# Second attention of a two-layer decoder, taken by batches within two pairs of heads, with the bidirectional attention of the first batch beside its last steps

## What is computed

```python
# experts: every expert on every token, weighted by its gate
h_mid = gelu(einsum('th,ehf->etf', x, moe_w1)); expert_out = einsum('etf,efh->eth', h_mid, moe_w2)
# layer 1, self-attention ("second attention"): 16 heads of 64
scores = einsum('bhqd,bhkd->bhqk', q, k) + position_bias
out = einsum('bhqk,bhkd->bhqd', softmax(scores), v); x = x + out @ wo
# layer 1, bidirectional attention: hc are the normed tokens, hq the 77 context rows
Sim = (hc @ w1)[:, :, None] + (hq @ w2)[:, None, :] + einsum('bid,bjd->bij', hc * w3, hq) + b_sim
hq_hat = einsum('bij,bjd->bid', softmax(Sim, 2), hq)
hc_bar = einsum('bi,bid->bd', softmax(max(Sim, 2), 1), hc)
x = x + concat([hc, hq_hat, hc * hq_hat, hc * hc_bar]) @ W_qv + b_qv
```

## Time and profile before

| | |
|---|---|
| runs shown | 509.86, 511.59, 510.97 us; median 510.97 |
| the profiled execution | 511.17 us, span 509.1 us |
| up to the last experts | 0 to 187 us |
| last experts, norm, first projections | 187 to 218 us |
| steps of the second attention with scores | 218 to 439 us |
| last steps, bidirectional attention | 439 to 478 us |
| norm and feed-forward | 478 to 509 us |

### The profile page before, as it was taken

One profiled execution on the slowest core, in us unless ns is written; L12 is line 12 of the kernel. 1 busy time (PEld: TensorE's weight loads), 2 busy tenths in 40 slices (PEclk: granted clock), 3 DMA queues, 4 the chain that ended last, 5 costly groups with the idle time before them and its releaser, 6 DMA issues.

```text
span 509.1 us, 12379 instructions
## 1 busy us (share of the span) xinstructions
PE 454.2 (89%) x4396; PEld 318.5 (63%) x4396; DVE 372.3 (73%) x1005; ACT 287.0 (56%) x618; POOL 122.3 (24%) x203
## 2 busy tenths in 40 slices
PE   3779878887787998599999999999999999999897
PEld 1234556666663766347676676677676767888756
DVE  3757858998767799677767778686777777447666
ACT  3752325564346796377767667676776766313460
POOL 5050000270014467102322243132311211111200
PEclk9979879998987999699999999999999999998999
DMA  7298914500000130100100000000000000000001
GB/s 214 59 98 98 101 14 140 181 4 1 0 2 23 41 103 1 32 1 1 32 4 1 1 15 15 0 0 0 0 0 0 1 1 3 1 2 1 1 0 42
DMA packets 15616, 15.74 MB, mean 31 GB/s; under 512 B 1348, under 2 KB 12859, under 8 KB 15579
## 3 DMA queue, kind: packets, MB, share of 16 engines
q1 hardware_dynamic: 15579, 15.24, 14.5%
HBM read 10.52 MB, written 4.72 MB: 30 GB/s over the span
## 4 chain that ended last, share of the span: by engine, by line
PE 71%; DVE 20%; ACT 4%; issue 3%; DMA 1%; DVEq 0%; SPq 0%; ACTq 0%
PE bank L865 16%; PE bank L1308 11%; PE bank L1261 9%; PE bank L1197 5%; PE bank L1302 5%; PE bank L1161 3%; PE bank L1148 3%; PE bank L1211 3%; PE bank L1193 2%; DVE PX L1608 2%; DVE mx L1606 2%; PE bank L974 1%; PE bank L1420 1%; PE bank L870 1%; DVE stats L1447 1%
## 5 line engine op out<-in xcount | busy, mean ns | idle before, releaser
L779 ACT ACTIVATE SN<-SN,nmx 128x512 f32<-128x512 f32 x128 | 92.9, 726 | 9.4 <-DVE nmx L1808 8.4
L528 POOL TENSOR_TENSOR CTX<-YT 128x128 f32 (+1 forms) x64 | 29.4, 459 | 197.2 <-DVE YT L1806 197.2
L865 PE MATMUL bank<-cs,SN 128*128 128x128 f32 x512 | 67.5, 274 | 1.6
L865 PEld LDWEIGHTS bank<-cs,SN 128*128 128x128 f32 x512 | 57.0, 141 | 17.2 <-issue 11.5
L1261 PE MATMUL bank<-TK,TQ 64*128 64x512 f16 x384 | 52.6, 380 | 0.0
L1793 DVE CUSTOM_DVE_ANT_0 SN<-bank,strip 128x512 f32<-128x512 f32 x64 | 43.3, 677 | 1.3 <-PE bank L1261 1.3
L1808 DVE CUSTOM_DVE_ANT_0 SN<-bank,strip 128x512 f32<-128x512 f32 x64 | 43.6, 682 | 0.0
L1801 DVE COPY PTO<-bank 128x512 f32<-128x512 f32 x32 | 22.1, 692 | 23.8 <-PE bank L1308 23.8
L1801 DVE COPY Z<-bank 128x512 f32<-128x512 f32 x32 | 22.1, 692 | 23.4 <-PE bank L1308 23.3
L787 ACT COPY PTO<-bank 128x512 f32<-128x512 f32 x32 | 18.8, 586 | 29.5 <-PE bank L1308 29.5
L787 ACT COPY Z<-bank 128x512 f32<-128x512 f32 x32 | 18.8, 586 | 27.3 <-PE bank L1308 27.3
(11 more groups left out here) (300 smaller groups left out, 906.3 us busy)
## 6 DMA issues: line engine op xcount, KB each, us to landing
bias_rows<-biasr SPq DMA_DIRECT2D x1, 4096.0 KB, 44.4
band<-bias_rows SPq DMA_DIRECT2D x1, 3072.0 KB, 13.0
wqkv<-in_twqkv SPq DMA_DIRECT2D x8, 192.0 KB, 2.7
w1s<-in_w SPq DMA_DIRECT2D x8, 128.0 KB, 2.3
w2s<-in_w SPq DMA_DIRECT2D x8, 128.0 KB, 2.1
wB<-in_wb SPq DMA_DIRECT2D x1, 753.0 KB, 6.2
wA<-in_wa SPq DMA_DIRECT2D x1, 520.0 KB, 5.2
X<-in_x SPq DMA_DIRECT2D x2, 256.0 KB, 3.2
```

The source lines that it names most:

```text
L779: sc.activation(p, p, ACT.Exp, bias=nmx[:, r % RING, h:h + 1], scale=-1.0, accum_out=psm[:, r % RING, h:h + 1]).then_inc(sm["exp_ready"], 1)
L865: return nc.tensor.transpose(out_, in_, ident[0:n, 0:n])
```

## The change

The rows are taken in groups of four: within two pairs first batch 0 of both, then batch 1 of both (where, pair_of). Projections come per group, three in four steps; only q, k and v of the first group stand ahead of or in step 0. The norm of batch 1 ahead of the attention, the last half output of expert 7 with its sum, and the high and low part of its input move into steps 0 to 3; the last expert is taken in halves of tokens, with 14 matmuls on ones between them. CTX and wo are kept as f16 high and low parts, so that GpSimd does three operations per row instead of one and an output tile is 24 f16 matmuls instead of 8 f32 ones. RAW moves from YT to wC. Output tiles 0 to 3 stand in steps 12 to 15 and 4 to 7 in steps 18 to 21 of the last pass; the norm, similarities, softmax and context of batch 0 stand between them in steps 15 to 21, and batch 1 alone follows. The bias b_qv is added into X by GpSimd.

```diff
-FIRST_OUT = ROWS + LAG
+OUT_TILE = {12: 0, 13: 1, 14: 2, 15: 3, 18: 4, 19: 5, 20: 6, 21: 7}
+OUT_BANK = (7, 7, 7, 7, 7, 3, 7, 5)
...
-PROJECTIONS = [("q", 0), ("k", 0), ("q", 1), ("k", 1), ("v", 0), ("v", 1)]
-JOBS = len(PROJECTIONS)
-SPLIT_JOBS = 4
+JOBS = 3
+LOWS = 2
+GROUPS = BODY // TG
 JOB_BANK = 7
-FIRST_BANKS = (6, 7, 4, 5, 6, 7)
-JOBS_FROM = 1
+FIRST_BANKS = (5, 3, 6)
+YP_BANK = (4, 6)
+LAST_ORDER = (0, 2, 1, 3)
...
-            CTX = t5("CTX", [P, PAIRS, TOK])
-            RAW = YT[:, :].rearrange("p (r c) -> p r c", c=2 * P)
+            CTX = t5("CTX", [P, PAIRS, 2, TOK], F16)
...
+            WOP = t5("WOP", [P, 2, PAIRS * P], F16)
+            RAW = wC[:, :].rearrange("p (r c) -> p r c", c=2 * P)
...
+            pool.wait_ge(sm["ld_band"], 16)
             for u in range(2):
                 for part in range(2):
                     split_part(0, u, part)
+                for part in range(6):
+                    strip_part(u, u, part)
+            wo = WO[:, :, :].rearrange("p n c -> p (n c)")
+            pool.wait_ge(sm["ld_wo"], 16)
+            gp.tensor_tensor(WOP[:, 0, :], wo, ones[:, 0:1].to_broadcast([P, PAIRS * P]), ALU.mult).then_inc(sm["ow_ready"], 1)
+            pool.wait_ge(sm["ow_ready"], 2)
+            gp.tensor_tensor(WOP[:, 1, :], wo, WOP[:, 0, :], ALU.subtract).then_inc(sm["ow_ready"], 1)
...
                     pool.wait_ge(sm["raw_ready"], n - 4)
-                    gp.tensor_tensor(dst, raw[:, 0:P], raw[:, P:2 * P], ALU.mult).then_inc(sm["ctt_ready"], 1)
+                    gp.tensor_tensor(CTW[:, :], raw[:, 0:P], raw[:, P:2 * P], ALU.mult).then_inc(sm["ctw_ready"], 1)
+                    pool.wait_ge(sm["ctw_ready"], 2 * n - 9)
+                    gp.tensor_tensor(dst[:, 0, :], CTW[:, :], ones[:, 0:1].to_broadcast([P, P]), ALU.mult).then_inc(sm["ctw_ready"], 1)
+                    pool.wait_ge(sm["ctw_ready"], 2 * n - 8)
+                    gp.tensor_tensor(dst[:, 1, :], CTW[:, :], dst[:, 0, :], ALU.subtract).then_inc(sm["ctt_ready"], 1)
...
-                    part = s - (LAG + 2 * u)
...
                     if part in (0, 1) and not last:
...
+                            pool.wait_ge(sm["pj_mm"], (i * GROUPS + u + 3) * JOBS)
...
+                    part = 2 * (s - (ROWS + TG * (u + 1) + 1))
...
+                if last and s == ROWS + TG + 6:
+                    add_bias(0)
+
+            def add_bias(g):
+                t = slice(TG * g, TG * g + TG)
+                pool.wait_ge(sm["ln_y"], TAIL + 1 + 2 * g)
+                b = row("b_qv").rearrange("p (o d) -> p o d", o=1).to_broadcast([P, TG, P])
+                gp.tensor_tensor(X[:, t, :], X[:, t, :], b, ALU.add).then_inc(sm["xb_ready"], 1)
...
+                for p in (2 * half, 2 * half + 1):
+                    gelu(NE - 1, p, LAST_ORDER[p])
+                for p in (2 * half, 2 * half + 1):
+                    high(NE - 1, 1, p, LAST_ORDER[p])
...
+            rstd_of(5, 0)
+            norm_high(0)
...
+                if s == 0:
+                    high_part(3, 2, 0, 0, FIRST_BANKS[2])
...
-                if last and s == FIRST_OUT + 4:
+                if s == 1:
+                    rstd_of(5, 1)
+                if s == 3:
+                    norm_high(1)
+                if last and s == 16:
+                    rstd_tiles(TAIL + 1, 0, TG)
+                if last and s == 17:
...
+                    take_tiles(1, 0, TG)
+                if last and s == 18:
+                    similarity_exp(0)
+                if last and s == 19:
+                    take_ast(0)
+                if last and s == 20:
+                    maxima_exp(0)
+                    take_context(0)
+                if last and s == 21:
                     rstd_tiles(TAIL + 2, TG, TG - 1)
...
-            similarity_exp(0)
-            take_tiles(2, TG, TG - 1, 3)
+            t5_steps(act, t5_step)
+            take_tiles(2, TG, TG - 1)
             rstd_tiles(TAIL + 3, NT - 1, 1)
-            take_tiles(3, NT - 1, 1, 4)
-            take_ast(0)
-            maxima_exp(0)
+            take_tiles(3, NT - 1, 1)
             similarity_exp(1)
-            take_context(0)
+            take_ast(1)
+            rstd_tiles(TAIL + 4, 0, TG)
             maxima_exp(1)
-            take_ast(1)
             take_context(1)
-
...
-            hidden(NE - 1, 1)
-            for u in range(2):
-                expert_out(NE - 2 + u, u)
...
+            last_hidden(0)
+            pe.wait_ge(sm["hid_lo"], (NE - 2) * 4 + 4 + 4)
+            pe.wait_ge(sm["acc_ready"], 2 * NE - 3)
+            half_out(NE - 2, 0, 0, 5)
+            last_hidden(1)
+            pe.wait_ge(sm["hid_lo"], (NE - 1) * 4 + 2 + 4)
+            half_out(NE - 1, 1, 0, 2)
...
+            keep_busy(0, 14)
+            pe.wait_ge(sm["acc_ready"], 2 * NE)
+            half_out(NE - 2, 0, 1, 6)
...
+            pe.wait_ge(sm["gel_ready"], NE * 4 + 4)
+            projected_norm(0)
+            pe.wait_ge(sm["hid_lo"], NE * 4 + 4)
+            half_out(NE - 1, 1, 1, 7)
+            pe.wait_ge(sm["ln_yt"], 9)
...
+                    pe.wait_ge(sm["to_ready"], 5 if tile == 6 else tile)
                 for p in range(PAIRS):
-                    ins = mm(bank[out_bank(tile)][:, 0:P], CTX[:, p, P * tile:P * tile + P], WO[:, p, :], start=(p == 0), stop=(p == PAIRS - 1))
+                    for k, (c_part, w_part) in enumerate(PRODUCTS):
+                        ins = mm(bank[OUT_BANK[tile]][:, 0:P], CTX[:, p, c_part, P * tile:P * tile + P], WOP[:, w_part, P * p:P * p + P],
+                                 start=(p == 0 and k == 0), stop=(p == PAIRS - 1 and k == 2))
                 ins.then_inc(sm["wo_mm"], 1)
...
+                if last and 12 <= s < 16:
+                    out_tile(OUT_TILE[s])
...
+                    turned(n, s)
+                if s == 3:
+                    pe.wait_ge(sm["pj_hi"], JOBS)
+                    projected_norm(1)
+                if s == 4:
+                    pe.wait_ge(sm["ln_yt"], 10)
...
+                if last and s == 16:
+                    pe.wait_ge(sm["ttr_ready"], PAIRS * ROWS * 2 - 2)
+                    mm(bank[1][0:1, 0:NG * XS], col("ws2"), wB_("ctxT", NG * XS), start=True, stop=True).then_inc(sm["rj_mm"], 1)
+                if last and s == 17:
+                    tiles_t(TAIL + 1, range(TG), ROWS_BANK[0])
+                if last and s == 18:
+                    pe.wait_ge(sm["rj_ready"], 2)
+                    bias_rows(0)
+                    pe.wait_ge(sm["ln_yt"], 10 + 1)
+                    similarity(0, range(TG))
+                if last and s == 19:
+                    maxima_t(0)
+                if last and s == 21:
+                    weighted_rows(0)
+                    pe.wait_ge(sm["to_ready"], 6)
+                    fused_context(0)
+                if last and s >= 18:
+                    out_tile(OUT_TILE[s])
+                if last and s == 19:
+                    attention_t(0)
+                    maximum_rows(0)
+                if last and s == 20:
+                    context_out(0)
...
-            tiles_t(TAIL + 2, PIECE_3, 3)
-            pe.wait_ge(sm["to_ready"], NT - 1)
-            maxima_t(0)
+            tiles_t(TAIL + 2, PIECE_3, ROWS_BANK[1])
+            fused_product(0, range(TG), False)
+            bias_rows(1)
             pe.wait_ge(sm["ln_yt"], 10 + 2)
             similarity(1, PIECE_3)
-            keep_busy(2, 2)
-            tiles_t(TAIL + 3, (NT - 1,), 4)
-            attention_t(0)
+            tiles_t(TAIL + 3, (NT - 1,), ROWS_BANK[2])
+            fused_rows(0, True)
             pe.wait_ge(sm["ln_yt"], 10 + 3)
             similarity(1, (NT - 1,))
-            maximum_rows(0)
-            keep_busy(7, 2)
-            context_out(0)
-            weighted_rows(0)
+            keep_busy(4, 6)
             maxima_t(1)
             attention_t(1)
-            fused_context(0)
             maximum_rows(1)
-            fused_product(0, range(TG), False)
-            fused_rows(0, True)
+            keep_busy(2, 2)
             context_out(1)
             weighted_rows(1)
+            pe.wait_ge(sm["to_ready"], NT)
             fused_context(1)
             fused_rows(1, False)
...
+            hidden_low(NE - 2, 0)
+            done = 2 * (NE - 3) + 2
+            gated_half(NE - 3, 0, 5, done + 3, done - 1)
+            hidden_low(NE - 1, 1, LAST_ORDER, (0, 1))
+            gated_half(NE - 2, 0, 5, done + 5, done + 1)
+            gated_half(NE - 1, 0, 2, done + 6, done + 2)
+            dve.wait_ge(sm["acc_ready"], done + 3)
             dve.sem_inc(sm["x_done"], 1)
             norm_stats(5, 0, X)
-            gated_sum(NE - 1, 1, (1,))
-            dve.wait_ge(sm["acc_ready"], 2 * NE + 2)
-            dve.sem_inc(sm["x_done"], 1)
-
-
-            dve.wait_ge(sm["x_done"], 4 + 2)
-            norm_stats(5, 1, X)
-            for g in range(NG):
-                norm_rows(5, g, X, Y)
-            for g in range(NG):
```

(72 more changed lines are left out.)

367 lines of the change are left out of this document (184 added, 183 removed).

## The result

The changed kernel takes 520.29 us (median of 4 runs, 519.71 to 520.87); the kernel before took 510.42 beside it. The ratio is 1.0197, 95% interval 1.0168 to 1.0225. I had forecast 516.0 and a range of 508 to 520: slower, as said, but by 9.9 us instead of 5.1, and 0.3 us outside the range. The profiled execution took 519.71 us with a span of 517.7, 8.6 more than before.

The account below looks back on a forecast made before the run. TensorE was taken to bound the attention steps, waits both ends. Start and middle -0.5, four tiles +1.6, steps 16 to 21 +7.0, behind tile 7 -2.1 and -0.9: +5.1 on 511.17 profiled, 516.2; median 516.0, range 508 to 520.

Parts of the forecast that it names:

- the waits named: Steps 16 to 21: TensorE waits for VectorE at row 14's copy and product copy, softmax weights and negated maximum.
- The middle: Step 5 to step 16: steps keep 3.14 and 3.65 us, three more projections inside steps cost 1.5, four tiles about 1.1.
- the tiles: Output tiles: 24 f16 matmuls take 1.4 us instead of 1.99 in f32; each adds 1.34 in steps 12 to 15.
- GpSimd's three products: Attention steps: three GpSimd products a row take 1.4 us, at most twice that, within a 3.14 us step, so cost zero.
- the stage behind tile 7: After the last output tile: 14.9 us to the last fused product, 2.1 less; then 4.8 to the input's maximum, 0.9 less.
- the step on the start: Start of the attention: the output weights' split, some 7 us on GpSimd, delays only GpSimd's first row product.
- the walk: VectorE's new order from 195.4 us: first scores at 211.3, 6.8 us earlier; step 5 at 229.2, 2.5 us earlier.
- the step of steps 16 to 21: Last attention steps: VectorE's order makes TensorE wait, so tile 7 ends 28.1 us after step 16 starts, 7.0 later.
- rival 3: TensorE's clock falls once for 6 us in the new waits of the last steps, adding 3 us: 519; chance 11%.
- Rival 1: Steps 16 to 21: no waits form, TensorE bounds the stage with 20.0 us of work, total 508; chance 26%.
- Rival 2: Steps 0 to 3: batch 1's norm fits VectorE's gaps, the start keeps 6.8 us instead of 2.5, total 511.9; chance 13%.
- Rival 4: GpSimd can't keep pace or tiles take their old price, +4.6 us on the tiles, total 520.5; chance 3%.

Follow-up runs that it names:

- the split moved: Changed kernel with GpSimd's two passes splitting the output weights moved from the start of the attention to step 7 of the last loop body: 512.7 us.
- the changed kernel's second trace: The changed kernel measured and profiled once more, unaltered: 521.1 us, ratio 1.0188 to the kernel before.
- the pieces of 128 columns: Changed kernel with the output weights' split left in place, each of its two 1024-column passes cut into eight instructions: 512.6 us.
- two details of its order put right: Changed kernel with the output weights' split in step 7 of the last body and VectorE's new order in steps 15 to 20: 506.1 us, again 507.4.
- the last two medians: Changed kernel with the split in step 7 and VectorE's new order, again: 507.4 us; the same with three more order edits at the end, again: 505.4.

## Why the prediction was right and wrong

**Right.** That it gets slower, and by which mechanism in the last steps: the waits named were there, at the product copy of row 14 (1.67 us, I had 1.9), the softmax weights (1.49, 1.7) and the negated maximum (0.90 with the split moved, 0.31 in the changed kernel's second trace, none in its first, where the half clock covers it), and a reordering of VectorE alone took these three away. The middle (+3.5, forecast +3.6), the tiles (1.51 us against my 1.4; in full steps +1.34 forecast, 4.46 - 3.14 = 1.32 measured), GpSimd's three products at zero, and the stage behind tile 7 (14.9 us to the last fused product, forecast 14.9; then 4.2 against 4.8). The last is in part luck: six of the twelve other traces had a fall of the clock in that stage, 1.3 us and more, for which I had no term.

**Wrong: the step on the start**, "The new split of the output weights ... delays only GpSimd's first row product". It costs 6.1 us at the first scores (5.2 in the second trace). I had cited the very rule: the Trainium skill (SBUF - State Buffer, section SBUF: two separate sides) says that such a lock is exclusive, for a whole instruction. I bounded its cost by "one such stall of 1.1 us", the duration of another pair's stall. By the rule the stall lasts as long as the other engine's instruction still runs, and I had that priced too, at some 3.5 us for each of the two passes; what I didn't do was to ask which VectorE instructions stand beside them. Two did (1.94 and 2.60 us), 3.5 us in all, and the lower clock that follows added 2.5. The trace agrees with the rule, as both stalls end with the pass beside them, and the pieces of 128 columns, which take the loss away, confirm it. Without the passes the walk was good: first scores 21.9 us behind expert 6 against the 22.8 of my walk; step 5 at 38.3 against 40.7, so there I gave back 2.4 too much.

**Wrong: the step of steps 16 to 21, in size.** "Tile 7 ends at t = 28.1" left out the clock. Without a fall it ends at 26.2, 29.2 less the 3.0 us from the last scores to step 16. So the waits were 1.9 over-priced, mostly in allowances before tile 4, which ended at 12.1 instead of 13.2; the fall came on top with 3.7 (1.1 in the second trace; rival 3, to which I gave 11% and 3 us). The rows that spoke for it were there: 0.50 and 0.59 in the kernel before. It deserved more than 11%.

The sum in my own terms: +5.1 forecast; +6.1 for the passes, -2.4 for the start without them, +3.7 for the fall, -1.9 for the waits, -0.6 behind tile 7, +0.9 near the end, where TensorE's filler and the feed-forward's first products run at the lower clock in this trace; -0.1 in the middle. That gives 10.8 us; the traces have 8.6 + 2.1 = 10.7 behind expert 6, the medians 9.9.

**The rivals.** Rival 1 (TensorE bounds the stage) is what VectorE's new order makes of it: 21.1 us behind step 16, where I had reckoned 20.0 for TensorE alone. It was not the kernel as written. Rival 2 (the start keeps its gain) isn't it either: with the moved split 4.9 us are kept of 7.6 at the first scores, between my 2.5 and the rival's 6.8, so VectorE's queue did give a part back. Rival 4 fell: tiles of 1.51 and unchanged steps. With two details of its order put right the change gains 0.7 to 0.8% on the kernel before; they cost 14 us.

**Open.** Why the clock falls in the changed kernel's last steps and not with the moved split, whose waits there are the same, was not settled, nor why it falls behind tile 7 in the variants where it doesn't fall in the last steps; nor how much of the 2.1 us between the last two medians is order and how much clock (in their traces about 1.9 us is order, 1.3 clock). Waits alone don't explain a fall: in the kernel before the clock fell near 467 us, with no idle stretch of TensorE over 0.3 us in the 6 us ahead of it.

## What to carry to other kernels

Where work is moved to an idle engine, list what its neighbour executes in the same microseconds: where both read SBUF the price is up to the whole instruction of the other, so cut long GpSimd passes into pieces, or put them beside steps in which VectorE reads PSUM. When a stage is interleaved with another, put into each queue first what another engine waits for, and sums, stats and copies behind it; here that order alone was worth 8 us. Where several waits of 1 to 2 us follow each other, put a fall of TensorE's clock into the sum with a real chance, and make filler no longer than the wait.

## What was not expected of the hardware

- A VectorE instruction with one tensor and two column operands in SBUF (the norm row) waits as well: 1.94 us beside GpSimd's 1.89. In the small it shows beside GpSimd's copies and products in general: rows of 0.43 to 0.52 us where one alone takes 0.31 to 0.35.
- The same 2 x 1024 columns take GpSimd 4.0 us beside VectorE's PSUM work (1.89 and 2.14), 4.5 at the start, and 6.9 in 16 pieces there. The pass of 2.58 at the start began beside a low part of VectorE that took only 0.68: it seems to have waited for that in its turn.
- A filler product of ones (128 x 128, f32, two records) takes 0.25 us at the upper clock.
- Without any difference in the code ahead of it, expert 6's hidden products start up to 3.1 us apart from trace to trace, while from there to step 5 the six traces without the passes at the start and with batch 1's norm in the steps lie at 38.3 or 38.4, and from step 5 to the last scores all lie at 208.2 (f32 tiles 210.3). Marks inside the kernel settled here what the totals couldn't.
